# Node pass of a four-layer graph network: a norm on ScalarE, a bias sum on POOL, index transfers spread anew

## The reference, cut to what matters

```python
h = relu(layernorm(x)); x = x + gat(h, ...)      # 5 attention layers on 25000 edges, biases added, relu between them
h = relu(layernorm(x)); x = x + hgt(h, ...)      # a * (gelu(out) @ Wa + ba) + (1 - a) * h
h = relu(layernorm(x)); x = x + gcn(h, ...)      # gelu(sum(h[src] * norm) @ W + b), self loops in the sum
h = relu(layernorm(x)); x = x + cat(h, ...)      # typed attention + h @ W[0] + bias
```

## Time and profile before

| | |
|---|---|
| median of the timed runs | 5280.24 us |
| span of the profiled execution, first to last instruction | 5284.5 us |
| instructions | 101919 |
| TensorE matmul / weight load busy | 4281.1 us (81%) / 3707.5 us (70%) |
| VectorE busy | 4007.8 us (76%) |
| ScalarE busy | 3358.8 us (64%) |
| POOL busy | 3254.8 us (62%) |
| node pass, from first to last power of line 479 | 107.56 to 1576.32 us |
| mean granted TensorE clock | 0.880 |

### The profile page before, as it was taken

The page is one execution under the profiler, slowest core; times in us unless marked ns, Lnnn a source line. Parts: engine busy times, 40 slices in busy tenths (PEclk is TensorE's granted clock), DMA queues, the critical chain, the costliest instruction groups (busy, mean ns, idle before and its releaser), DMA issues. The chain is left out here.

```text
span 5284.5 us, 101919 instructions
## 1 busy us (share of the span) xinstructions
PE 4281.1 (81%) x28013; PEld 3707.5 (70%) x28013; DVE 4007.8 (76%) x15157; ACT 3358.8 (64%) x9065; POOL 3254.8 (62%) x2905
## 2 busy tenths in 40 slices
PE   4899999999976978969969958776895858869575
PEld 4777777778865867858858847644775847757475
DVE  5799999999976766767757767787676959859765
ACT  2788887888855866847847847643873537758400
POOL 2888888878877727637457367222761257566277
PEclk6999999999988989989989979855997979989755
DMA  3999876665645636636636546487773759847332
GB/s 92 187 219 217 220 218 212 222 219 206 212 150 125 143 85 133 135 77 142 128 90 141 110 107 142 110 246 225 169 153 90 196 141 248 236 114 132 74 94 85
DMA packets 1107280, 825.56 MB, mean 156 GB/s; under 512 B 209510, under 2 KB 1068202, under 8 KB 1106396
## 3 DMA queue, kind: packets, MB, share of 16 engines
q1 hardware_dynamic: 1026800, 690.47, 48.7%
q0 software_dynamic: 77040, 128.08, 12.0%
q10 hardware_dynamic: 2880, 0.50, 0.1%
HBM read 374.78 MB, written 448.11 MB: 156 GB/s over the span
## 5 line engine op out<-in xcount | busy, mean ns | idle before, releaser
L805 POOL DMA_INDIRECT gat_G<-table,k_src_row x980 | 1071.7, 1094 | 316.6 <-issue 282.5
L1598 ACT ACTIVATE gat_Gw<-gat_G,gat_al 128x128 f32<-128x128 f32 x1960 | 618.5, 395 | 89.0 <-DVE gat_al L1423 89.0
L1454 DVE SCALAR_TENSOR_TENSOR gat_Gw<-gat_own,gat_al,gat_Gw 128x128 f32<-128x128 f32 x1960 | 555.3, 344 | 70.5 <-ACT gat_Gw L1598 70.3
L1715 PE MATMUL gat_psG<-gat_ends_at,gat_Gw 128*128 128x128 f32 x3920 | 536.4, 281 | 42.3 <-DVE gat_Gw L1454 42.2
L1743 PE MATMUL gat_psZ<-gat_aggT,t_gat_wh 128*128 128x256 f32 x1960 | 525.5, 391 | 16.5 <-ACT gat_hT L1624 16.1
L1715 PEld LDWEIGHTS gat_psG<-gat_ends_at,gat_Gw 128*128 128x128 f32 x3920 | 491.9, 197 | 53.3 <-DVE gat_Gw L1454 50.1
L635 PEld LDWEIGHTS nodes_psR<-t_ident_v,nodes_hTl 128*128 128x128 f32 x3168 | 435.3, 193 | 106.0 <-issue 1.8
L635 PE MATMUL nodes_psR<-t_ident_v,nodes_hTl 128*128 128x132 f32 x3168 | 450.5, 279 | 0.0
L479 POOL TENSOR_TENSOR nodes_rstd<-nodes_var,k_half 128x14 f32<-128x14 f32 x140 | 367.7, 2626 | 116.0 <-DVE nodes_var L546 116.0
L1624 ACT ACTIVATE gat_hT<-gat_psZ,t_gat_bias 128x256 f32<-128x256 f32 x490 | 231.6, 473 | 266.4 <-PE gat_psZ L1744 263.4
L1743 PEld LDWEIGHTS gat_psZ<-gat_aggT,t_gat_wh 128*128 128x128 f32 x1960 | 338.6, 193 | 57.9 <-ACT gat_aggT L1605 18.7
(11 more groups left out here) (668 smaller groups left out, 12635.5 us busy)
## 6 DMA issues: line engine op xcount, KB each, us to landing
table<-nodes_rows SPq DMA_DIRECT2D x660, 198.0 KB
table<-nodes_n SPq DMA_DIRECT2D x396, 192.0 KB
gat_own<-table SPq DMA_DIRECT2D x490, 132.0 KB
table<-gat_rows SPq DMA_DIRECT2D x392, 132.0 KB
nodes_x<-in_x SPq DMA_DIRECT2D x132, 192.0 KB
out<-nodes_x_out SPq DMA_DIRECT2D x132, 192.0 KB
gat_G<-table,k_src_row POOLq DMA_INDIRECT x980
hgt_q<-enter_q SPq DMA_DIRECT2D x98, 144.0 KB, 2.2
```

What stands on the lines that cost most here:

```text
L805: eng.indirect_dma_start(to, None, table, bass.IndirectOffsetOnAxis(ap=index, axis=0)).then_inc(sem, 16)
L1454: ins = eng.scalar_tensor_tensor(Gw[:, i % RS, t, h, :], own[:, i % RO, t, 0:D], al[:, g % 2, 1, a:a + 1], Gw[:, i % RS, t, h, :], ALU.mul ...
L1598: ins = eng.activation(Gw[:, i % RS, t, h, :], G[:, i % RG, t, 0:D], ACT.Copy, scale=al[:, g % 2, 0, a:a + 1])
L1715: mm = eng.matmul(o[:, h * P:(h + 1) * P], Gw[:, i % RS, t, h, :], ends_at[:, i % RE, t, :], start=True, stop=True)
```

## The change

ScalarE computes `n1` as three activations `Identity(x1 * rstd + shift)` ahead of `h5c`, which from then on waits for ScalarE's own `nB1`; VectorE no longer does. Because VectorE's x1 buffer is now read by ScalarE, the sum `x1` waits for the norm two blocks back. `shift` is made in four more steps, from a mean in place of a negated one, and the small sums on VectorE shrink from six instructions to five. The sum that adds `cat_b` to `xs` moves from VectorE to the end of POOL's step, behind a wait for `n3`. The row-map transfers are issued 2.5 a step (two and three by turns) up to step 97 and 4 a step from step 98, so that they last to step 134 instead of 130.

```diff
--- before.py
+++ after.py
@@ -345,8 +345,8 @@
         xg = A.sb("xg", [P, SG, SC, D])
         srows = A.sb("srows", [P, RB, SC, ROWW])
         st = A.sb("st", [P, 2, M, 6])
-        diff, total, spread2, square = (A.sb(m, [P, M]) for m in ("diff", "total", "spread2", "square"))
-        negmean, var, rstd = (A.sb(m, [P, 4, M]) for m in ("negmean", "var", "rstd"))
+        diff, spread2, square = (A.sb(m, [P, M]) for m in ("diff", "spread2", "square"))
+        mean, var, rstd = (A.sb(m, [P, 4, M]) for m in ("mean", "var", "rstd"))
         shift = A.sb("shift", [P, 4, M])
         hT0 = A.sb("hT0", [P, W])
         hTl = [None] + [A.sb(f"hTl{l}", [P, W]) for l in range(1, L)]
@@ -470,7 +470,8 @@
                     eng.tensor_tensor(xb[:, b % XB, :, :], x[:, b % XB, :, :], spread(last_b[:, :], 1, T), ALU.add).then_inc(s.xb, 1)
 
                 steps = [("put", c) for c in range(C)] + [("got", c) for c in range(C)] 
-                per = (len(steps) + N - 1) // N
+                early = NS * 5 // 2
+                due = [min(len(steps), 5 * k // 2 if k <= NS else early + 4 * (k - NS)) for k in range(LAST + 2)]
                 gather_slots(0)
                 gather_slots(1)
                 for k in range(LAST + 1):
@@ -479,7 +480,7 @@
                         eng.tensor_tensor(rstd[:, k % 4, :], var[:, k % 4, :], K.half[:, 0:M], ALU.pow).then_inc(s.pow, 1)
                     if is_slots(k + 2):
                         gather_slots(k + 2)
-                    for what, c in steps[k * per:(k + 1) * per]:
+                    for what, c in steps[due[k]:due[k + 1]]:
                         if what == "put":
                             eng.indirect_dma_start(K.row_of, bass.IndirectOffsetOnAxis(ap=K.node_tm[:, c:c + 1], axis=0),
                                                    K.slot_row_tm[:, c:c + 1], None, bounds_check=K.rows - 1,
@@ -490,6 +491,13 @@
                             gather(eng, K.row_of, K.src_tm[:, c:c + 1], K.src_row[:, c:c + 1], s.row_got)
                     if is_block(k):
                         with_bias(k)
+                    b = k - 8
+                    if is_block(b):
+                        if b == 0:
+                            eng.wait_ge(s.bias_in, 32)
+                        eng.wait_ge(s.nC, b + 1)
+                        eng.tensor_tensor(xs[:, b % SB, :, :], xs[:, b % SB, :, :], spread(cat_b[:, :], 1, T), ALU.add
+                                          ).then_inc(s.x3b, 1)
                     if N <= k < N + 8:
                         c = (k - N) * 25
                         eng.tensor_tensor(K.dinv[:, c:min(c + 25, C + 2)], K.deg[:, c:min(c + 25, C + 2)],
@@ -520,8 +528,8 @@
 
                 def normed(k, to, of, at, m, sem):
                     for t in range(m):
-                        ins = eng.tensor_scalar(to[:, t, 0:D], of[:, t, :], negmean[:, k % 4, at + t:at + t + 1],
-                                                rstd[:, k % 4, at + t:at + t + 1], ALU.add, ALU.mult)
+                        ins = eng.tensor_scalar(to[:, t, 0:D], of[:, t, :], mean[:, k % 4, at + t:at + t + 1],
+                                                rstd[:, k % 4, at + t:at + t + 1], ALU.subtract, ALU.mult)
                     ins.then_inc(sem, 1)
 
                 n_stats += stats_of_x(0)
@@ -537,20 +545,20 @@
                         eng.wait_ge(s.stats, n_stats)
                         eng.tensor_tensor(diff[:, :], mean0, mean1, ALU.subtract).then_inc(s.small, 1)
                         eng.scalar_tensor_tensor(square[:, :], sq0, float(D) * LN_EPS, sq1, ALU.add, ALU.add).then_inc(s.small, 1)
-                        eng.tensor_tensor(total[:, :], mean0, mean1, ALU.add).then_inc(s.small, 1)
                         eng.wait_ge(s.small, n_small + 1)
                         eng.scalar_tensor_tensor(spread2[:, :], diff[:, :], 0.25, diff[:, :], ALU.mult, ALU.mult).then_inc(s.small, 1)
+                        eng.scalar_tensor_tensor(mean[:, k % 4, :], diff[:, :], 0.5, mean1, ALU.mult, ALU.add).then_inc(s.small, 1)
                         eng.wait_ge(s.small, n_small + 3)
-                        eng.tensor_scalar(negmean[:, k % 4, :], total[:, :], -0.5, None, ALU.mult).then_inc(s.small, 1)
-                        eng.wait_ge(s.small, n_small + 4)
                         eng.scalar_tensor_tensor(var[:, k % 4, :], square[:, :], 1.0 / D, spread2[:, :], ALU.mult, ALU.add
                                                  ).then_inc(s.var, 1)
-                        n_small += 5
+                        n_small += 4
 
                     b = k - 3
                     if is_block(b):
                         eng.wait_ge(s.mixed4, b + 1)
                         eng.wait_ge(s.xb, b + 1)
+                        if b >= 2:
+                            eng.wait_ge(s.nB1, b - 1)
                         eng.tensor_tensor(x1[:, b % 2, :, :], wide(psX), xb[:, b % XB, :, :], ALU.add).then_inc(s.x1, 1)
                     if is_block(k + 1):
                         n_stats += stats_of_x(k + 1)
@@ -580,13 +588,9 @@
                     if k < N + 8:
                         eng.wait_ge(s.small, n_small)
                         eng.wait_ge(s.pow, k + 1)
-                    if is_block(k):
-                        eng.tensor_tensor(shift[:, k % 4, :], negmean[:, k % 4, :], rstd[:, k % 4, :], ALU.mult).then_inc(s.shift, 1)
-                    b = k - 4
-                    if is_block(b):
-                        if b >= RB:
-                            eng.wait_ge(st5[b % RB], 16 * (b // RB))
-                        normed(k, n1[:, b % RB, :, :], x1[:, b % 2, :, :], at_1, T, s.nB1)
+                    if k < N + 4:
+                        eng.scalar_tensor_tensor(shift[:, k % 4, :], mean[:, k % 4, :], -1.0, rstd[:, k % 4, :], ALU.mult, ALU.mult
+                                                 ).then_inc(s.shift, 1)
                     b = k - 5
                     if is_block(b):
                         if b >= RB:
@@ -601,11 +605,6 @@
                     if is_block(b):
                         eng.tensor_tensor(xs[:, b % SB, :, :], x1[:, b % 2, :, :], spread(K.hgt_ba[:, :], 1, T), ALU.add
                                           ).then_inc(s.x1b, 1)
-                    b = k - 8
-                    if is_block(b):
-                        eng.wait_ge(s.nC, b + 1)
-                        eng.tensor_tensor(xs[:, b % SB, :, :], xs[:, b % SB, :, :], spread(cat_b[:, :], 1, T), ALU.add
-                                          ).then_inc(s.x3b, 1)
                     b = k - 4
                     if is_block(b):
                         eng.wait_ge(s.h5c, b + 1)
@@ -756,6 +755,14 @@
                                        ).then_inc(s.scoresS_out, 1)
                     c = k - 4
                     if is_block(c):
+                        eng.wait_ge(s.shift, k + 1)
+                        if c >= RB:
+                            eng.wait_ge(st5[c % RB], 16 * (c // RB))
+                        for t in range(T):
+                            ins = eng.activation(n1[:, c % RB, t, :], x1[:, c % 2, t, :], ACT.Identity,
+                                                 bias=shift[:, k % 4, at_1 + t:at_1 + t + 1],
+                                                 scale=rstd[:, k % 4, at_1 + t:at_1 + t + 1])
+                        ins.then_inc(s.nB1, 1)
                         eng.wait_ge(s.nB1, c + 1)
                         eng.activation(h5c[:, c % 2, :, :], n1[:, c % RB, :, :], ACT.Relu, scale=K.hgt_gate[:, 1:2]
                                        ).then_inc(s.h5c, 1)
```

## The result

The changed kernel takes 5446.4 us (median of four runs, 5444.45 to 5455.71), the kernel before beside it 5285.0: a ratio of 1.0314, 95% interval 1.0294 to 1.0334. It is 161 us slower (forecast 207). The profiled execution spans 5453.8 us, 169.3 more than that of before, and is read here. All of it lies in the node pass; the table cuts that at the first matmul of steps 9, 98 and 132 and at the first matmul behind the pass.

What follows compares the result with a forecast made beforehand. The prediction took the node pass to be bound by a TensorE, ScalarE, TensorE ring; 148 + 13 + 2 + 2 + 42 = 207 us on 5280 gave 5487 us, with an 8-in-10 range of 5375 to 5640.

Steps and rivals of the forecast that it cites:

- The ring: Node pass, chain TensorE, ScalarE, TensorE closing each step: the norm adds 1.32 us, giving 12.27 with slots, 10.87 without.
- the hand-over to the ReLU: ScalarE's wait on its own semaphore between the moved norm and the ReLU: 0.06 us, bounds nothing and 0.2.
- VectorE's share: VectorE's 91% busy time in slot steps, cited for the rival that VectorE was the bound: 5260 us, chance 0.05.
- The small excess of before: Steps 9 to 97 before the change: mean 11.08 us, 0.13 above 10.95, put down to POOL running late now and then.
- The clock: TensorE's longer stands bring half clock in one slot step in three: 30 x 1.40 = 42 us; none without slots.
- 10 of 18: Before the change, warm pass: of 18 TensorE stands of 0.9 to 1.6 us before a transposition, 10 were followed by half clock.
- the rival of that name: TensorE's clock falls in nearly every step of the node pass: 165 + 122 x 1.40 = 336 us, 5616 us; chance 0.12.
- POOL: POOL's chain in the node pass: 11.4 us with slots, 10.6 or 11.5 without, counted as nothing; rival bound 5358 to 5387, chance 0.08.
- The end of the pass: From step 132, transfers lasting to step 134 cost 13 us, POOL's adds of steps 135 to 139 another 2.
- The beginning: First steps: fewer transfers help POOL in steps 0 to 3, the norm costs from step 4: together +2 us.
- Identity on ScalarE: The norm's activation function needs no other table set, so nothing; rival with table loads: 339 us more, 5826 us, chance 0.01.

Runs made afterwards that it cites:

- the norm alone: Changed kernel with the last bias sum back on VectorE and row-map transfers back to three a step: 5431.4 us, ratio 1.0284.
- the run that only relieved it: Kernel before, with VectorE making one tile of three of the first post-attention norm and of the last bias sum, the rest left out: 5273.0 us, ratio 0.9987.
- POOL's sum gone: Kernel before with only the sum of the first layer's bias (xb) moved from POOL to VectorE: 5267.9 us, ratio 0.9979.
- The moved turn: Kernel before with TensorE's turn of the first norm's rows put ahead of the product of line 684 and its row product: 5545.7 us.
- the two lengthened norms: Changed kernel with the norm's three activations all made twice on ScalarE: 5698.5 us; with only one of them made twice: 5617.4 us.
- the run with the new spread alone: Kernel before with only the row-map transfers respread, 2.5 a step up to step 97, then 4: 5313.7 us, ratio 1.0053.
- POOL's part alone: Changed kernel with the first post-attention norm n1 put back on VectorE, bias sum on POOL and new transfer spread kept: 5345.2 us, ratio 1.0128.

## Why the prediction was right, point by point

**The ring.** It gave 12.27 and 10.87 us a step; the trace has 12.23 and 10.85. The three activations take their 1.26 us; the hand-over to the ReLU on the same engine, taken at 0.06, is 0.03 (1271.50 to 1271.53). The sum for steps 9 to 131, 148 us, is met by 105.6 + 42.6 = 148.2, and nearly by the norm alone (105.1 + 40.7). That it is met to 1 us is in part luck: about 5 us of the 148.2 are half clock, so the ring itself has 143. One row was misread: the 0.33 us for which TensorE was said to idle without slots are idle time of the weight load, and the matmuls of that turn stood less; after the change their stand is 1.49 us, not 1.6. That VectorE's share was no guide is shown by the run that only relieved it.

**The small excess of before.** The mean of 11.08 against the ring's 10.95 was put down to POOL running late. The origin was right; how it costs was not seen. Seven steps of 12.28 to 12.96 us carry 10.7 of the 12 us, each with a stand of 0.9 to 1.6 us for the second norm, and half clock behind it as here (timeline row and window of the kernel before):

```profile
443.96 0.55 PE L627 MATMUL nodes_psB<-k_ident,nodes_n 128*128 128x128 f32 x3 [0.98 <-DVE nodes_n L523]
...
444.60:447.00 2.40, 2.40 (x17) 2.40 (x16) 2.04 (x6) 2.15 (x7) 1.92 (x2) 0.65 0.99 317
```

With POOL's sum gone the mean was 10.96.

**The clock, the term that was mis-sized.** The prediction counted 30 falls of 1.40 us in the steps with slots, +42. The price of a fall was somewhat high: behind a stand of 1.92 us at 401.74 two steps took 13.16 and 12.76 us, 1.44 together above 12.24, but 0.25 of that is the longer stand; the second fall, at 1211.25, cost 1.15 in the same way. The number was wrong: there are two such falls in steps 9 to 97, and all that those steps have above 89 x 12.235 is 3.2 us. Without slots, where none was counted, there was one: 12.73 us in place of 10.85, behind a stand of 1.96 us for the second norm (1601.62). The failing step was to throw stands of all places together ("10 of 18"): eight of those ten stood behind the score matmuls, and the new stand stands behind a full product. The moved turn shows that the place matters, the two lengthened norms that the length does. Nor was the forecast's other side far: one more activation of 0.4 us brought half clock in each step with slots and in every second one without. That this gave 5617 us, and the rival of that name 5616, is chance, since 50 of it are the activation itself.

**POOL.** With slots it was given 11.4 us with its wait and called no bound: right. Without slots it counted nothing against 10.87, on the ground that the stretched transfers would go back: they did (0.95 us each in the changed kernel, 1.81 with the norm on VectorE), and VectorE's blocked instruction is one with time behind it. Alone, POOL's part is dear, +67.

**The end of the pass.** +15 forecast, +17.7 measured. The transfers are 12.8 of it by the run with the new spread alone (13 forecast), so the second sum and what else lies there have 4.9 in place of 2. The prediction let that sum find VectorE's third norm "done long before POOL gets there"; from step 135 POOL stood 6.8 us for it.

**The beginning.** +5.2 for +2. The norm brings it: with the norm alone step 9 begins at 209.42, with POOL's part alone at 199.01. Both traces of the table have half-clock steps there, that of before one of 15.63 us (step 7) that most of the other runs lack, so the difference is uncertain by some us.

**Identity on ScalarE** needed no other table set: in the changed kernel's trace no table load lies between 99.8 and 1758.3 us, that is in the whole pass, as the Trainium skill (ScalarE: Activation LUTs, Table sets) had it. The median moved by 161 us and the profiled span by 169; the forecast's 207 less the 39 us of missing falls (42 less 3.2) is 168; the smaller misses above cancel.

## What to carry to other kernels

Read which engine's wait closes the ring before work is moved to a less busy engine: ScalarE had 20% idle time and VectorE 9%, yet 1.3 us on ScalarE cost 1.3 us a step and relief on VectorE brought 7 us in all. Where a step has two bounds of one length, mend both in one version, since each alone shows little (5 us, not clear of nothing, and 12 us alone, 59 together). Cost a sum on POOL by what it blocks on VectorE: here moving one from POOL to VectorE gained, and the change had moved one the other way.

## What the runs showed of the hardware

- TensorE's clock fell to 0.50 behind stands of 0.90 to 1.96 us that followed the score matmuls and the turn, or the score matmuls alone, often but not each time (eight of 14 in the kernel before, none of 30 without slots in the run with the new spread). In steps 9 to 131, behind a full product and its row product, it stayed at 1.00 after stands of 1.33 to 1.68 us, fell after two of four of 1.91 to 1.95, after each of 2.05, and after every second one of 2.82 up to step 64.
- A POOL indirect transfer took longer by about the length of the VectorE sums in a row that began with it: 2.38 us against three, 1.81 against two, 0.95 against none. A lone sum that began 0.28 or 0.50 us into a transfer left it at 0.94 and 0.99 (changed kernel, transfers at 1492.99 and 1490.44). The Trainium skill (SBUF — State Buffer, Who interferes with whom) infers that sums of this kind leave descriptor generation alone; the lengthened transfers differ from that, and no run here shows why.
- A small VectorE difference that starts 0.02 us ahead of two POOL sums ends only with them, 2.02 us in place of 0.17.
- ScalarE's hand-over to itself through a semaphore costs 0.03 us (1271.50 to 1271.53). A score copy that just misses its input starts 0.16 us later than a ready instruction would (0.56 against 0.40 behind the start of the one ahead), and this shows as no idle time.
